# Second attention of a fused kernel: heads projected eight at a time, and values products of two key tiles issued together

## The reference

```
q = einsum('ble,fe->blf', x, q_w) + q_b          # 8 x 512 x 256
v = einsum('bce,fe->bcf', cross, v_w) + v_b      # 8 x 1024 x 256
q, v = reshape to (b, 16 heads, ., 16)
scores = einsum('bhld,bhcd->bhlc', q, v) / sqrt(16)
out = einsum('bhlc,bhcd->bhld', softmax(scores), v)
return einsum('ble,fe->blf', out, o_w) + o_b
```

## Time and profile before

| | |
|---|---|
| median of three runs | 3473.93 us |
| the profiled execution: its time, its span | 3477.76 us, 3475.9 us |
| busy in the span: PE, PEld, DVE, ACT, POOL | 94%, 54%, 68%, 48%, 37% |
| second attention, first to last max product | 2178.4 to 3223.7 us of the span |
| PE row of `a_m<-a_vh,a_qz` L1391 | 1024 matmuls, mean 467 ns, 466.1 us busy |
| PE row of `a_t<-a_qs,a_vs` L1411 | 1024 matmuls, mean 397 ns |
| PE row of `a_o<-a_prob,a_v_all` L1418 | 2048 rows, mean 599 ns |
| DVE row of `a_mhalves<-a_m` L1657 | 1024 reduces, mean 687 ns, idle before them 182.5 us |
| weight loads of L1391 waiting for DVE's reduces | 248.7 us, 391 times |

### The profile page before, as it was taken

One profiled execution on the slowest core, in us unless ns is written; L12 is line 12 of the kernel. 1 busy time (PEld: TensorE's weight loads), 2 busy tenths in 40 slices (PEclk: granted clock), 3 DMA queues, 4 the chain that ended last, 5 costly groups with the idle time before them and its releaser, 6 DMA issues. The chain is left out here.

```text
span 3475.9 us, 46403 instructions
## 1 busy us (share of the span) xinstructions
PE 3260.8 (94%) x14300; PEld 1888.5 (54%) x14300; DVE 2353.9 (68%) x3720; ACT 1666.7 (48%) x1899; POOL 1296.5 (37%) x609
## 2 busy tenths in 40 slices
PE   6999999999999999999999878899999999999678
PEld 4556556555565565565565455455555555555357
DVE  4675674675656756746746434778778788777679
ACT  3443443443434434434434322466566566565378
POOL 1664774665746647646746623000000000000102
PEclk9999999999999999999999989899999999999788
DMA  6554553545455544545535242343344344344202
GB/s 182 124 141 114 122 140 100 136 112 132 113 131 120 135 119 116 130 112 136 139 94 126 59 130 83 87 101 99 88 101 103 82 103 108 77 103 93 82 4 94
DMA packets 265143, 379.61 MB, mean 109 GB/s; under 512 B 35945, under 2 KB 170673, under 8 KB 265009
## 3 DMA queue, kind: packets, MB, share of 16 engines
q1 hardware_dynamic: 265008, 378.06, 43.7%
HBM read 82.22 MB, written 27.26 MB: 31 GB/s over the span
## 5 line engine op out<-in xcount | busy, mean ns | idle before, releaser
L863 POOL TENSOR_TENSOR a_prob_sum<-a_prob_sum,a_prob 128x1024 f32<-128x1024 f32 x384 | 923.9, 2406 | 115.5 <-ACT a_prob L588 90.2
L588 ACT ACTIVATE a_prob<-a_t 128x1024 f32<-128x1024 f32 x512 | 517.8, 1024 | 743.9 <-PE a_t L433 736.5
L1657 DVE TENSOR_REDUCE a_mhalves<-a_m 128x1 f32<-128x512 f32 x1024 | 689.5, 687 | 182.5 <-PE a_m L1391 179.5
L731 DVE TENSOR_REDUCE a_mhalves<-a_m 128x1 f32<-128x512 f32 x1024 | 688.3, 689 | 172.5 <-PE a_m L397 159.5
L1557 ACT ACTIVATE a_prob<-a_t 128x1024 f32<-128x1024 f32 x512 | 500.0, 1023 | 168.5 <-PE a_t L1411 162.7
L440 PE MATMUL a_o<-a_prob,a_v_pair 128*64 128x512 f32 x2048 | 496.9, 606 | 0.0
L1391 PE MATMUL a_m<-a_vh,a_qz 128*128 128x512 f32 x1024 | 466.1, 467 | 27.0 <-DVE a_mhalves L1657 18.7
L397 PE MATMUL a_m<-a_kh_n,a_qz 128*128 128x512 f32 x1024 | 408.0, 429 | 21.5 <-DVE a_mhalves L731 9.7
L863 POOL TENSOR_TENSOR a_prob_sum<-a_prob 128x1024 f32<-128x1024 f32 x64 | 151.6, 2368 | 592.4 <-ACT a_prob L588 592.4
L1391 PEld LDWEIGHTS a_m<-a_vh,a_qz 128*128 128x128 f32 x1024 | 191.1, 189 | 319.1 <-DVE a_mhalves L1657 248.7
L425 PE MATMUL a_t<-a_q_hl,a_k_hh 128*128 128x512 f32 x1024 | 334.5, 408 | 10.5 <-DMA a_k_hh<-a_kh_n 10.2
(11 more groups left out here) (256 smaller groups left out, 4077.7 us busy)
## 6 DMA issues: line engine op xcount, KB each, us to landing
a_k_hh<-a_kh_n SPq DMA_DIRECT2D x256, 256.0 KB, 4.5
a_k_lm<-a_kl_n SPq DMA_DIRECT2D x128, 256.0 KB, 4.9
a_v_pair<-a_v_all SPq DMA_DIRECT2D x64, 512.0 KB, 5.2
a_vs<-a_vh SPq DMA_DIRECT2D x256, 128.0 KB, 2.3
a_wk<-wk_parts SPq DMA_DIRECT2D x64, 256.0 KB, 2.9
a_q_hl<-a_qz SPq DMA_DIRECT2D x128, 128.0 KB, 2.4
a_q_hm<-a_qz SPq DMA_DIRECT2D x128, 128.0 KB, 2.4
a_q_hl<-a_ql_n SPq DMA_DIRECT2D x128, 128.0 KB, 2.4
```

Of the source, the lines that this page charges most:

```text
L588: nc.scalar.activation(prob[:, t % RING], ps_t[t % 2][:, :, :], ACT.Exp, scale=SCALE0).then_inc(s_exp, 1)
L731: nc.vector.tensor_reduce(mhalves[:, qt, hd, n:n + 1], ps_m[:, n, :], AX.X, ALU.max).then_inc(s_max, 1)
L863: nc.gpsimd.tensor_tensor(acc, prob[:, (t - 1) % RING] if t == 1 else acc, prob[:, t % RING], ALU.add).then_inc(s_acc, 1)
L1657: nc.vector.tensor_reduce(mhalfs[:, u, qt, h, k:k + 1], ps_m[:, k, :], AX.X, ALU.max).then_inc(s_max, 1)
```

## The change

Inside `second_attention` only:

- A projection now covers eight heads, unpadded (16 columns for each head, 128 partitions), for two groups. `project(k, c)` belongs to block k = G // 2. Even groups project the queries of block G // 2 + 1 (in the gap behind the values products of tiles 2 and 3), odd groups the two halves of the values of block (G + 3) // 2 (behind those of tiles 0, 1 and of tiles 2, 3). Each group thus has either 2 query matmuls or 10 value matmuls, not both. `split_high` and `split_low` go with them: one before reduce 25 in even groups, two before reduces 14 and 25 in odd ones.
- `probs_v` is called for two key tiles in a row, and `prob` has four slots instead of three. The order of scores and max products around them is another.
- The last max product stands right ahead of `max_rows`, and the values products 6 and 7 behind it.
- `spread` and `stack` copy 16 rows a head instead of 32, in as many DMAs; `vs` and `qs` are filled with zeros first by POOL; the padded weights and their splits at the start are gone; the next batch's context is loaded at a batch's start.

The diff, cut to what matters:

```diff
-        RB = 3
+        RB = 4
...
-        LOWS = (11, 20, 29)
+        V_LOWS = (14, 25)
+        Q_LOW = 25
+        TURNS_KEPT, V_KEPT, Q_KEPT = (1, 3), (3, 5), 5
+        TURNS, V_AT, Q_AT = (0, 1), (1, 3), 4
...
-            def project(G, n, c, between=None, bank=None):
-
-                if bank is None and c > 0:
-
-                    pe.wait_ge(s_lo, 3 * G + c)
+            def project(k, c, between=None, bank=None):
+
+                if bank is None and c == 1:
+
+                    pe.wait_ge(s_lo, 3 * k + 1)
                 out = ps_x[:] if bank is None else bank
+                cols = slice(P * (k % 2), P * (k % 2 + 1))
                 if c < 2:
                     keys = slice(c * 512, (c + 1) * 512)
                     for step, (context, piece, rows) in enumerate(ctx_weights):
-                        mm = pe.matmul(out, wvp[0:rows, piece, n, :], context[:, keys],
+                        mm = pe.matmul(out, wv[0:rows, piece, cols], context[:, keys],
                                        start=(step == 0), stop=(piece == 3))
                         if between and step == 2:
                             between(1)
                     mm.then_inc(s_kq, 1)
                 else:
-                    pe.matmul(out, wqp[:, 0, n, :], xnT[:, 0, :], start=True, stop=False)
+                    pe.matmul(out, wq[:, 0, k % 2, :], xnT[:, 0, :], start=True, stop=False)
                     if between:
                         between(1)
-                    pe.matmul(out, wqp[:, 1, n, :], xnT[:, 1, :], start=False, stop=True).then_inc(s_kq, 1)
+                    pe.matmul(out, wq[:, 1, k % 2, :], xnT[:, 1, :], start=False, stop=True).then_inc(s_kq, 1)
...
-                ahead = n < NG - 2 or left
+
+                block = (G + 3) // 2 if n % 2 else G // 2 + 1
+                ahead = block < 2 * B
+
+                def pieces(t):
+
+                    if ahead and n == 2 and t in TURNS:
+
+                        if t == TURNS[1]:
+                            pe.wait_ge(s_xnT, DCH * (b + 1) + 1)
+                        turn_queries(b + 1, TURNS.index(t))
+                    if ahead and n % 2 == 0 and t == Q_AT:
+                        if n == 2:
+
+                            pe.wait_ge(s_xnT, DCH * (b + 2))
+                        project(block, 2, maxima)
+                        maxima(1)
+                    if ahead and n % 2 and t in V_AT:
+                        if n == 1:
+                            pe.wait_ge(s_ctx, 48 * (b + 2))
+                        project(block, V_AT.index(t), maxima)
+
                 maxima(2)
                 pe.wait_ge(s_st[u], STACK * (2 * b + n // 2 + 1))
-                for t in range(KT):
-
-                    odd = t in (1, 3, 5)
-                    if odd:
+                for t in range(0, KT, 2):
+                    for v in (t, t + 1):
+                        if v:
+                            maxima(1)
+                        scores(G, u, v, 0)
                         maxima(1)
-                    scores(G, u, t, 0)
-                    maxima(1)
-                    scores(G, u, t, 1)
-                    if t < KT - 1:
+                        scores(G, u, v, 1)
+                        if v == 1:
+                            maxima(1)
+                            pieces(0)
+                    if t:
                         maxima(1)
-                    if t == 1:
+                    if t == 2:
 
                         pe.wait_ge(s_oraw, G)
-                    if t >= 1:
+                    if t:
+                        probs_v(G, n, t - 2)
                         probs_v(G, n, t - 1)
-                        if t < KT - 1:
+                        if t < KT - 2:
+                            maxima(2)
+                            pieces(t - 1)
                             maxima(1)
-                    if ahead and n == 2 and t in (0, 2):
-
-                        if t == 2:
-                            pe.wait_ge(s_lo, 3 * (G + 2) + 1)
-                        turn_queries(b + 1, t // 2)
-                    if odd:
-                        if ahead:
-                            if n == 2 and t < 5:
-
-                                pe.wait_ge(s_xnT, DCH * (b + 1) + t // 2 + 1)
-                                pe.wait_ge(s_ctx, 48 * (b + 2))
-                            project(G + 2, (n + 2) % NG, t // 2, maxima)
-                        else:
+                            pieces(t)
                             maxima(1)
-                        maxima(1)
-                assert not todo
+                maxima(len(todo))
                 if n < NG - 1 or left:
                     if ahead:
 
-                        pe.wait_ge(s_lo, 3 * (G + 3))
+                        pe.wait_ge(s_lo, 3 * block + (2 if n % 2 else 3))
                     max_rows(G + 1, (n + 1) % 2)
+                probs_v(G, n, KT - 2)
                 probs_v(G, n, KT - 1)
 
...
-            def split_high(G, n, c, bank=ps_x[:]):
-
-                u = n % 2
-                act.wait_ge(s_kq, 3 * G + c + 1)
-                out = vh[:, u, c * 512:(c + 1) * 512] if c < 2 else qh[:, u, :]
+            def split_high(k, c, bank=ps_x[:]):
+
+                act.wait_ge(s_kq, 3 * k + c + 1)
+                out = vh[:, k % 2, c * 512:(c + 1) * 512] if c < 2 else qh[:, k % 2, :]
                 nc.scalar.activation(out, bank, ACT.Identity,
-                                     bias=(bvp if c < 2 else bqp)[:, n:n + 1]).then_inc(s_hi, 1)
+                                     bias=(bvp if c < 2 else bqp)[:, k % 2:k % 2 + 1]).then_inc(s_hi, 1)
 
...
-                    if ahead and n == 2 and t in (0, 2):
-                        keep_turned(b + 1, t // 2)
-                    if ahead and t in (1, 3, 5):
-                        split_high(G + 2, (n + 2) % NG, t // 2)
+                    if ahead and n == 2 and t in TURNS_KEPT:
+                        keep_turned(b + 1, TURNS_KEPT.index(t))
+                    if ahead and n % 2 == 0 and t == Q_KEPT:
+                        split_high(block, 2)
+                    if ahead and n % 2 and t in V_KEPT:
+                        split_high(block, V_KEPT.index(t))
...
+                lows = {} if not ahead else dict(zip(V_LOWS, range(2))) if n % 2 else {Q_LOW: 2}
                 if n < NG - 1 or left:
                     for c in range(CMB):
                         if c == 2 and n > 0:
                             keep_o(G - 1)
                         if c == 5 and n > 0:
                             divide(G - 1, n - 1)
-                        if ahead and c in LOWS:
-                            if c == LOWS[0]:
-
-                                dve.wait_ge(s_st[u], STACK * (2 * b + n // 2 + 1))
-                            split_low(G + 2, (n + 2) % NG, LOWS.index(c))
+                        if c in lows:
+                            split_low(block, lows[c])
                         take_max(G + 1, (n + 1) % 2, c)
...
-            fills = [(wvp[DC1:P, 3].bitcast(F32), 0.0), (wv[DC1:P, 3].bitcast(F32), 0.0),
-                     (qz[:].bitcast(F32), 0.0), (mcol[:, :, 0:3 * QD].bitcast(F32), 0.0),
-                     (qs[3 * QD:P, 0].bitcast(F32), 0.0), (qs[3 * QD:P, 1].bitcast(F32), 0.0),
+            fills = [(wv[DC1:P, 3].bitcast(F32), 0.0), (qz[:].bitcast(F32), 0.0),
+                     (vs[0:3 * QD, 0].bitcast(F32), 0.0), (qs[:, 0].bitcast(F32), 0.0),
+                     (mcol[:, :, 0:3 * QD].bitcast(F32), 0.0),
+                     (vs[0:3 * QD, 1].bitcast(F32), 0.0), (qs[:, 1].bitcast(F32), 0.0),
                      (v_all[:, :, :, HD1:VW], 0.0), (v_all[:, :, :, HD1:HD1 + 1], 1.0)]
...
```

More of the change, by code:

```diff
@@ L1741, in _ @@
             dve.wait_ge(s_const, 16 * NCONST)
-            split_low(0, 0, 0, first_banks[0])
-            split_weights((2, 3))
-            for c in (1, 2):
-                split_low(0, 0, c, first_banks[c])
+            for c in range(3):
+                split_low(0, c, first_banks[c])
             nc.vector.memset(ps_o[:], 0.0).then_inc(s_oz, 1)
@@ L1750, in _ @@
                 if c - 3 in FIRST_PROJECTIONS:
-                    split_low(1, 1, FIRST_PROJECTIONS.index(c - 3))
+                    split_low(1, FIRST_PROJECTIONS.index(c - 3))
                 take_max(0, 0, c)
@@ L2309, in layouts @@
     inner = H0 * HD0
-    def pad(v):
-        out = np.zeros((v.shape[0], H1, QD), v.dtype)
-        out[:, :, :HD1] = v.reshape(v.shape[0], H1, HD1)
-        return out.reshape(v.shape[0], H1 * QD)
     return {
```

137 lines of the change are left out of this document (62 added, 75 removed).

## The result

The changed kernel takes 3574.57 us (median, 3573.56 to 3576.89) where the kernel before, on the same chip, takes 3474.38 (3473.51 to 3475.70): 1.0289 times as long, 95% interval 1.0271 to 1.0307. The forecast was 3569. The profiled execution has a span of 3571.7 us, 95.8 more than before.

The account below looks back on a forecast made before the run. PE looked full, but DVE's reduces behind two banks were taken to bind in the new order: 87 + 8 + 0 = +95 on 3477.8, 3573, medians 3.8 lower, so 3569 us; own range 3535 to 3595, overall 3485 to 3608.

Parts of the forecast that it names:

- opening: A group's start up to its first values product: 8.55 us, or 8.06 in the first group of a batch.
- turns with values: Odd groups' turns that each project half of the values: 10.2 us the first, where split_low waits, 9.4 the second.
- end of a group: Last two pairs of values products with max_rows between, max_rows 1.5 behind max product 32: 5.75 us in sum.
- PE's own saving: Work PE no longer does: 2.0 us from projections and 1.2 from paired values products, 3.2 a group.
- start-up: Before the groups: POOL's zero fills against no query projection for the second block; taken as 0, bounds -4 and +8.
- The walk: One group of the second attention followed by prices from rows of before: odd 33.9 us, even 33.4, first of a batch 32.9.
- The sum: Whole kernel: seven batches +87, last batch +8, start-up 0, total +95 us on the profiled execution's 3477.8.
- DVE sets its length: In a group's opening, DVE's 11 reduces and 1.25 us of other work were said to set the stretch's length.
- First rival: DVE keeps up and PE's saving of 99 us is all realised: 3375 us; chance 0.10.
- Second rival: Only DVE's chain counts, waits for exponentials and split_high hide in it: +0.5 us a group, 3489 us; chance 0.09.
- Third rival: Each group's bunch of five max products lowers PE's clock for one turn: +62 us, 3628; chance 0.07.
- PE's busy share: In the groups, PE busy some 80%, named as a sign that the forecast was right.

Follow-up runs that it names:

- e3: The changed kernel with the 32nd max product issued ahead of the last pair of values products but one: 3534.15 us.
- e5: The changed kernel with each reduce reading 256 of the 512 columns, 422 ns instead of 688: 3508.99 us.
- e11: The kernel before with the new projection, four prob slots and paired values products, but the order of before: 3483.72 us.
- e13: e10 with one max product more between the two key tiles of a turn and the low parts one reduce later: 3471.39 us.
- e10: The changed kernel with the 32nd max product early, split_low later and the divide before reduce 11 instead of 5: 3504.59 us.
- e1: The kernel before with the new projection and four prob slots, single values products and the order of before: 3449.10 us.
- e14: e1 with one of three max products in a row issued between the second and third head of the values product ahead: 3483.39 us.
- e2: The kernel before with values products of two key tiles back to back, its projection and three prob slots kept: 3510.65 us.

## Why the prediction was right

By its own steps, measured in the group shown above and in its neighbours:

| step | predicted | measured |
|---|---|---|
| opening, n odd; first of a batch | 8.55; 8.06 | 8.56; 8.09 |
| opening, n = 2 | 8.55 | 8.81 to 8.84 |
| turn with five max products | 8.3 | 8.28 |
| turn with the queries | 10.8 | 10.82 |
| turns with values, first; second | 10.2; 9.4 | 10.13; 9.34 |
| end of a group | 5.75 | 5.73 |
| a batch | 144.3 (+12.5) | 144.4 (+12.4) |
| PE's own saving, a group | 3.2 | 3.2 (2.5, 0.4 within projections, 0.3 behind values products) |
| reduces across a pair | 2.30 apart | 2.27 |
| start-up | 0 (-4 to +8) | about -2 |
| clock | 1.00 in all groups | once at 0.50 in each of three groups |

- **The walk** held within 0.1 us at each step but one, because every price in it was a distance between starts in rows of before, and because it followed three engines at once. Of its long waits, that of `max_rows` was put at "1.5 behind max 32" and is 1.59; e3 shows that it was worth 40 us. The step that is off is the opening of the group n = 2, 0.3 longer: the walk has no step for the next batch's queries, which PE turns there.
- **The sum** came out in its parts on the profiled executions: +95.8 against +95. The seven batches were 87 and are 87.5, the last batch 8 and is 9.2, and of what was put at nothing the start-up won 4.2 and the part behind the last `max_rows` lost 3.3. That these last two nearly cancel is luck. The clock's dips, some 5 us for which the sum has no term, are in these numbers. The 5.6 us between 3569 and 3574.57 come almost whole from the last step, which took 3.8 off because the medians of before lie under its profiled execution: of the changed kernel the median lies 1.0 above it.
- **The cause** was put too simply in one place. "DVE sets its length", said of the opening, is wrong: with halved reduces an odd group's opening is only 0.7 of its 8.56 us shorter, and ACT's exponentials then set it. (No run shortens the exponentials themselves; this is read from the trace of e5.) Nor is DVE's pace the main cause of the loss: reduces of 0.42 us for 0.69 take 20 of the 100 us between the two kernels away. What is left is the ways there and back: product, reduce and product through two banks; scores, exponentials and scores; projection, high part, low part, reduce and max product. The walk contained all of them, the sentence did not.
- **First rival** (DVE keeps up, 3375): PE's saving was there, all of the 3.2, but hardly any of it showed as time in the orders tried. With the same work e11 stands at 3484 and e13 at 3471.
- **Second rival** (only DVE's chain, 3489): e11 and e13 come near its time, once the waits for exponentials and the high part are few. That its mechanism holds there is not shown. In the changed kernel's own order these waits are not hidden.
- **Third rival** (the clock): the granted clock was 1.00 in the groups but for four single short dips to its lower level of 1.2 GHz, of which the last of the stretches above is one (0.50 at 2758.82). Two of them lie in an odd group's first turn with values, at a max product that had waited 1.34 us; these groups took 34.7 us instead of 33.7 and 33.8. The other two lie at the last two `max_rows`, where the pair behind takes 3.16 and 3.56 us instead of 1.91. That is some 5 us in all, not 62. The same waits stand in the other groups without a dip, and why these four have one, the trace does not tell; in e3 and e10, where `max_rows` does not wait, no group had one once the start-up's low clock had ended. (The rival's own sum, 3569 + 62, is 3631 and not 3628.)
- **A sign that I had wrong**: PE's busy share was to fall to 80%. It is 29.71 of 33.77, 88%, since a matmul that starts after a wait has a row of 0.50 for a price of 0.23: rows that overlap in a dense run stand apart in a thin one. The distances between starts say 24.9 of 33.7, 74%.
- **Start-up**: the fills did not hurt much. The four scalings took 9.66 instead of the 7.97 of the earlier trace rows, but the first `max_rows` came 4.2 earlier, of which 2.4 was already there when the stage began.

## What to carry to other kernels

When two engines hand work back and forth through two buffers, what a change does to the order can count for more than what it does to the instruction count. Here 27 us were won by the smaller projection, and 125 lost by putting what remained in lumps (e1 against the changed kernel): 35 by the pairs, 91 by the rest of the order. Price a new order by walking one period with starts, on all engines in the chain, and look first at what covers each way there and back, above all at the last item of a period. An engine that idles in front of its busiest instruction (182.5 us became 296.9) told of this loss where the busy shares hardly moved.

## What the runs showed of the hardware that I had not expected

- Four matmuls of 18 columns on four column groups of the array start 0.007 us apart and take 0.98 together, from the start to the next product; two of them take 0.97. The Trainium skill, TensorEngine Tiling (Array Packing), section Key Properties, says that different tiles can execute in parallel; the trace agrees, and e14 adds the price of using only half of them: nothing is saved.
- A change between those column groups and the whole array costs 0.10 ahead and 0.10 behind; the 0.10 behind stands behind every wait of PE too. Two values products back to back take 1.84 to 1.87, so pairing saves 0.9 us of PE's own a group (e2 against before, e11 against e1), and 0.3 more that the table counts with the waits: the 1.2 of the prediction.
- From a max product's start to its reduce's it is 0.54, from the reduce's end to the next product in that bank 0.05; the third product of a row is 0.71 late with a reduce of 0.69, 0.45 with one of 0.42.
